# A differential-attention kernel: bit operations in VectorE's exponential, a bias tile in ScalarE's, and 222 shares for 204

## The reference

```python
scores = einsum('bhtd,bhsd->bhts', q * hd ** -0.5, k)   # 32 heads, 2048 x 2048, four batches
attn_w = softmax(scores, axis=-1)
aw = attn_w[:, :, 0] - lam * attn_w[:, :, 1]
attn = einsum('bhts,bhsd->bhtd', aw, v)                  # then RMS norm, subln_w, Wo
```

## Time and profile before

| | us |
|---|---|
| median of 3 runs | 3611.6 (3609.43 to 3613.68) |
| the profiled execution | 3607.35 |
| its span, first to last instruction | 3605.5 |
| ScalarE busy | 3534.4 (98%) |
| of that in the loop's exponentials | 3497.4 |
| TensorE busy | 3405.9 (94%) |
| VectorE busy | 2588.9 (72%) |
| GpSimd busy | 338.0 (9%) |
| mean granted TensorE clock | 0.998 |

### The profile page before, as it was taken

The page is one execution under the profiler, slowest core; times in us unless marked ns, Lnnn a source line. Parts: engine busy times, 40 slices in busy tenths (PEclk is TensorE's granted clock), DMA queues, the critical chain, the costliest instruction groups (busy, mean ns, idle before and its releaser), DMA issues. The chain is left out here.

```text
span 3605.5 us, 76890 instructions
## 1 busy us (share of the span) xinstructions
PE 3405.9 (94%) x32302; PEld 799.1 (22%) x32302; DVE 2588.9 (72%) x3808; ACT 3534.4 (98%) x2808; POOL 338.0 (9%) x229
## 2 busy tenths in 40 slices
PE   8999999999899999999999999999999999989998
PEld 5222112122122222222222222222221222211222
DVE  6687878863578687776367768677547888878886
ACT  5999999999999999999999999999999999999998
POOL 3010101010010100101001010100100000000001
PEclk9999999999999999999999999999999999999999
DMA  6111110111101111101111001111012110010000
GB/s 196 28 32 39 32 31 22 35 39 33 38 21 42 48 35 40 50 23 33 36 47 50 25 31 36 40 49 36 20 31 63 45 37 22 17 30 16 20 22 26
DMA packets 103700, 136.90 MB, mean 38 GB/s; under 512 B 9916, under 2 KB 88716, under 8 KB 103340
## 3 DMA queue, kind: packets, MB, share of 16 engines
q1 hardware_dynamic: 102524, 131.01, 12.9%
q10 hardware_dynamic: 816, 0.79, 0.1%
HBM read 72.50 MB, written 59.19 MB: 37 GB/s over the span
## 5 line engine op out<-in xcount | busy, mean ns | idle before, releaser
L1146 ACT ACTIVATE probs<-ps 128x1536 f32<-128x1536 f32 (+1 forms) x2732 | 3497.4, 1670 | 15.5 <-PE ps L1263 13.9
L1291 PE MATMUL ps<-probs,values 128*32 128x512 f32 x14600 | 2047.9, 606 | 4.9 <-DVE wmod_sb L1644 2.4
L1263 PE MATMUL ps<-queries,keys 25*128 25x512 f16 x7680 | 1003.9, 385 | 160.6 <-ACT probs L1146 142.0
L1263 PEld LDWEIGHTS ps<-queries,keys 25*128 25x128 f16 x7680 | 249.8, 91 | 1947.3 <-ACT probs L1146 1861.5
L1291 PEld LDWEIGHTS ps<-probs,values 128*32 128x32 f32 x14600 | 300.2, 108 | 416.9 <-issue 410.5
L1623 DVE TENSOR_SCALAR d_y<-ps 128x512 f32<-128x512 f32 x240 | 165.6, 690 | 295.4 <-PE ps L1263 284.7
L1708 DVE STREAM_TRANSPOSE seg_t<-ps 128x512 f32<-128x512 f32 x127 | 91.0, 716 | 356.9 <-PE ps L1291 356.4
L1060 POOL TENSOR_TENSOR seg_rs<-seg_ms,neg_half 128x16 f32<-128x16 f32 x64 | 185.7, 2901 | 1506.1 <-DVE seg_ms L1721 1506.1
L1640 DVE SCALAR_TENSOR_TENSOR wmod_sb<-wmod_sb 128x1024 f32<-128x1024 f32 x204 | 249.6, 1224 | 6.3
L1644 DVE SCALAR_TENSOR_TENSOR wmod_sb<-wmod_sb,gates 128x1024 f32<-128x1024 f32 x204 | 249.5, 1223 | 6.0
L1642 DVE SCALAR_TENSOR_TENSOR wmod_sb<-wmod_sb,d_y 128x1024 f32<-128x1024 f32 x204 | 249.3, 1222 | 5.3
(11 more groups left out here) (181 smaller groups left out, 1690.9 us busy)
## 6 DMA issues: line engine op xcount, KB each, us to landing
v_scr<-a_v SPq DMA_DIRECT2D x16, 1024.0 KB, 5.6
values<-v_scr SPq DMA_DIRECT2D x29, 512.0 KB
queries<-q_scr SPq DMA_DIRECT2D x116, 96.0 KB
keys<-k_scr SPq DMA_DIRECT2D x116, 96.0 KB
e_x<-in_x_dram SPq DMA_DIRECT2D x18, 512.0 KB, 5.2
attn_scr<-seg_o SPq DMA_DIRECT2D x254, 32.0 KB
e_attn<-attn_scr SPq DMA_DIRECT2D x31, 256.0 KB, 3.6
out_dram<-e_y SPq DMA_DIRECT2D x15, 512.0 KB, 3.3
```

The source lines that it names most:

```text
L1146: nc.scalar.activation(probs[:, s % PRING, at, :], ps[:, base + at.start:base + at.stop:at.step, :], ACT.Exp, scale=1.0 / SQUARE).then_inc ...
L1263: last = nc.tensor.matmul(ps[:, score_bank(n), :], keys[buf][at, u * P:(u + 1) * P], queries[buf][at, tc * CH:(tc + 1) * CH], start=True, ...
L1291: last = nc.tensor.matmul(pv[row:row + VW, :], values[buf][:, n % SEG_BANKS // HEADS, j // 2, :], probs_of(n), start=(i == 0), stop=(i == ...
```

## The change

Three things are changed together.

1. **VectorE's exponential.** The read now multiplies by log2(e) x 2^23 and writes int32, so that the bits of the result are split into a whole and a fractional part. A share then has six instructions instead of seven: two bit operations of the kind TENSOR_SCALAR, and four SCALAR_TENSOR_TENSOR for a polynomial of degree 6 in all. Before there were two TENSOR_SCALAR and five SCALAR_TENSOR_TENSOR. The result comes out eight times as large.
2. **ScalarE's exponential** has to carry the same factor. It gets `bias=eight[:, 0:1]`, log 8 in a new 128 x 1 tile that GpSimd sets at the start, on every one of the 2732 ACTIVATEs.
3. **The plan.** `shared(k)` compares with 8 instead of 5: 18 segments have two shares instead of one, 222 shares in all and 444 slots. They are segments 25 and 26 of the first batch, and 1, 2, 9, 10, 17, 18, 25 and 26 of the second and the third. `SHARE_COST` has the six parts.

```diff
-POLY = [-2.135305643081665, 4.020981311798096, 4.626499652862549, -0.9490653276443481]
-SHIFT = 1.2185084819793701
...
-ROUND = 1.5 * 2.0 ** 21
-QUARTER_LOG2E = float(np.log2(np.e) / 4.0)
+POLY = [-0.9341297723814943, 2.4233820625103575, 5.176821583615651, 1.7852414559499343]
+POLY_SCALE = 0.2812099198503226
+EIGHT = float(np.log(8.0))
+WHOLE_BITS, PART_BITS, PART_SIGN = 0x7F800000, 0x007FFFFF, -0x41800000
...
+LOG2E_BITS = float(np.log2(np.e) * 2.0 ** 23)
...
-    D_LINKS = 6
+    D_LINKS = 5
...
-        return 2 if sum(light.get(step, 3) for step in steps) <= 5 and not normed else 1
+        return 2 if sum(light.get(step, 3) for step in steps) <= 8 and not normed else 1
...
-    SHARE_COST = (695, 1230, 695, 1225, 1225, 1225, 1225)
+    SHARE_COST = (695, 695, 1225, 1225, 1225, 1225)
...
+            nc.gpsimd.memset(eight[:, :], EIGHT).then_inc(eight_set, 1)
...
+            act.wait_ge(eight_set, 1)
             for s in range(ALL_SLOTS):
...
-                nc.scalar.activation(probs[:, s % PRING, at, :], ps[:, base + at.start:base + at.stop:at.step, :], ACT.Exp, scale=1.0 / SQUARE).then_inc(exp_done, 1)
+                nc.scalar.activation(probs[:, s % PRING, at, :], ps[:, base + at.start:base + at.stop:at.step, :], ACT.Exp, bias=eight[:, 0:1], scale=1.0 / SQUARE).then_inc(exp_done, 1)
...
-                V.tensor_scalar(block_y(j)[:, half * CH:(half + 1) * CH], ps[:, score_bank(n), :], EXP_LOW * SQUARE, QUARTER_LOG2E / SQUARE, ALU.max, ALU.mult).then_inc(d_read, 1)
+                V.tensor_scalar(block_y(j)[:, half * CH:(half + 1) * CH].bitcast(I32), ps[:, score_bank(n), :], EXP_LOW * SQUARE, LOG2E_BITS / SQUARE, ALU.max, ALU.mult).then_inc(d_read, 1)
...
-                    link.then(V.tensor_scalar(d_n, y, ROUND, -ROUND, ALU.add, ALU.add))
+                    link.then(V.tensor_scalar(d_n.bitcast(I32), y, WHOLE_BITS, WHOLE_FLIP, ALU.bitwise_and, ALU.bitwise_xor))
                 elif part == 1:
-                    link.then(V.scalar_tensor_tensor(d_y[:, :], d_n, SHIFT, y, ALU.subtract, ALU.subtract))
+                    link.then(V.tensor_scalar(d_y[:, :].bitcast(I32), y, PART_BITS, PART_SIGN, ALU.bitwise_and, ALU.bitwise_or))
                 elif part == 2:
-                    link.then(V.tensor_scalar(d_n.bitcast(mybir.dt.int32), d_n, BIAS, 2.0 ** 25, ALU.add, ALU.mult))
+                    link.then(V.scalar_tensor_tensor(d_y[:, :], d_y[:, :], POLY[0], d_y[:, :], ALU.add, ALU.mult))
                 elif part == 3:
-                    link.then(V.scalar_tensor_tensor(out, d_y[:, :], -POLY[0], d_y[:, :], ALU.add, ALU.mult))
+                    link.then(V.scalar_tensor_tensor(out, d_y[:, :], POLY[1], d_y[:, :], ALU.add, ALU.mult))
                 elif part == 4:
-                    link.then(V.scalar_tensor_tensor(out, out, POLY[1], out, ALU.add, ALU.mult))
-                elif part == 5:
                     link.then(V.scalar_tensor_tensor(out, out, POLY[2], d_y[:, :], ALU.add, ALU.mult))
                 else:
-                    V.scalar_tensor_tensor(out, out, -POLY[3], d_n, ALU.add, ALU.mult).then_inc(d_done, 1)
+                    V.scalar_tensor_tensor(out, out, POLY[3], d_n, ALU.add, ALU.mult).then_inc(d_done, 1)
```

More of the change, by code:

```diff
@@ L13 @@
 F16 = mybir.dt.float16
+I32 = mybir.dt.int32
 P = 128
-POLY = [-2.135305643081665, 4.020981311798096, 4.626499652862549, -0.9490653276443481]
-SHIFT = 1.2185084819793701
-LEAD = 1.3595123291015625
-BIAS = (126.0 + LEAD) / 4.0 - 64.0
-ROUND = 1.5 * 2.0 ** 21
-QUARTER_LOG2E = float(np.log2(np.e) / 4.0)
+POLY = [-0.9341297723814943, 2.4233820625103575, 5.176821583615651, 1.7852414559499343]
+POLY_SCALE = 0.2812099198503226
+EIGHT = float(np.log(8.0))
+WHOLE_BITS, PART_BITS, PART_SIGN = 0x7F800000, 0x007FFFFF, -0x41800000
+WHOLE_FLIP = 0x40000000 | int(np.float32(POLY_SCALE).view(np.int32)) & PART_BITS
+LOG2E_BITS = float(np.log2(np.e) * 2.0 ** 23)
 EXP_LOW = -87.0
@@ L341, in put @@
                 due = GROUP_SLOT.get(next(g for g in range(entry[1] // SEG_BANKS * NB, ALL_SEGS * NB) if entry[1] in group_banks(g)), ALL_SLOTS)
-                later.extend((due, 0, SHARE_COST[part], ("share", share, part)) for part in range(7))
+                later.extend((due, 0, SHARE_COST[part], ("share", share, part)) for part in range(6))
             elif entry[0] == "evacuate" and entry[1] == "a" and 2 <= entry[3] < 6:
@@ L467, in adaln_diff_attention @@
         neg_half = sb("neg_half", [P, 16])
+        eight = sb("eight", [P, 1])
         wq, wk, wv, wo, wf = (sb(f"w_{n}", [P, EC, E]) for n in ("q", "k", "v", "o", "f"))
@@ L609, in adaln_diff_attention @@
         consts_set = sem("consts_set")
+        eight_set = sem("eight_set")
         c_loaded = sem("c_loaded")
@@ L1062, in _ @@
                         held.append(task)
-                    elif what == "share" and task[1] == 6:
+                    elif what == "share" and task[1] == 5:
                         shares = task[0] + 1
@@ L1628, in share_part @@
                 j = share - SHARES[k]
-                link, y, out = Chain(dve, d_chain, share * D_LINKS + part), block_y(j), d_blocks[j]
+                link, y, out = Chain(dve, d_chain, share * D_LINKS + part), block_y(j).bitcast(I32), d_blocks[j]
                 if part == 0:
                     dve.wait_ge(d_read, 2 * (share + 1))
-                    link.then(V.tensor_scalar(d_n, y, ROUND, -ROUND, ALU.add, ALU.add))
+                    link.then(V.tensor_scalar(d_n.bitcast(I32), y, WHOLE_BITS, WHOLE_FLIP, ALU.bitwise_and, ALU.bitwise_xor))
                 elif part == 1:
-                    link.then(V.scalar_tensor_tensor(d_y[:, :], d_n, SHIFT, y, ALU.subtract, ALU.subtract))
+                    link.then(V.tensor_scalar(d_y[:, :].bitcast(I32), y, PART_BITS, PART_SIGN, ALU.bitwise_and, ALU.bitwise_or))
                 elif part == 2:
-                    link.then(V.tensor_scalar(d_n.bitcast(mybir.dt.int32), d_n, BIAS, 2.0 ** 25, ALU.add, ALU.mult))
+                    link.then(V.scalar_tensor_tensor(d_y[:, :], d_y[:, :], POLY[0], d_y[:, :], ALU.add, ALU.mult))
                 elif part == 3:
-                    link.then(V.scalar_tensor_tensor(out, d_y[:, :], -POLY[0], d_y[:, :], ALU.add, ALU.mult))
+                    link.then(V.scalar_tensor_tensor(out, d_y[:, :], POLY[1], d_y[:, :], ALU.add, ALU.mult))
                 elif part == 4:
-                    link.then(V.scalar_tensor_tensor(out, out, POLY[1], out, ALU.add, ALU.mult))
-                elif part == 5:
                     link.then(V.scalar_tensor_tensor(out, out, POLY[2], d_y[:, :], ALU.add, ALU.mult))
                 else:
-                    V.scalar_tensor_tensor(out, out, -POLY[3], d_n, ALU.add, ALU.mult).then_inc(d_done, 1)
+                    V.scalar_tensor_tensor(out, out, POLY[3], d_n, ALU.add, ALU.mult).then_inc(d_done, 1)
                     dve.wait_ge(d_done, share + 1)
```

## The result

The changed kernel takes 3841.6 us (median of 4, 3836.87 to 3844.03) against 3612.4 of the kernel before (median of 4). The ratio is 1.0634, 95% interval 1.0616 to 1.0653: slower by 6.3%. Forecast were 3835 us in a range of 3788 to 3862.

What follows compares the result with a forecast made beforehand. The prediction took ScalarE's chain of loop exponentials as the bound. From 3607.35 us it took 15.5 for narrow slots, added 246 for the operand and took 3 for TensorE: 3835 us, range 3788 to 3862.

Steps and rivals of the forecast that it cites:

- ScalarE as the bound: Loop: one chain of 2732 exponentials, 3497.4 us busy and 15.5 idle; changes to one ACTIVATE go nearly one for one into time.
- the operand: Loop exponentials on ScalarE: the bias as pointer operand adds 0.09 us to each of 2732, 246 us in all.
- The halving of the two-operand rows: ScalarE: ACTIVATEs with two pointer operands (bias and scale) cost 0.18 us more, so one operand was taken as 0.09.
- The narrow slots: ScalarE in the 18 added shares: 36 more slots with two banks instead of three, 0.43 us each, 15.5 us less.
- TensorE: Loop: 0.09 us more in each slot removes some short ScalarE waits for scores, 3 us of 15.5 taken off.
- The argument on the clock: TensorE: granted clock at the upper level in all 40 slices, even one where it is half busy; no reason for lower.
- VectorE at nothing: VectorE's shares: new arithmetic and 18 more shares, 111 us less to 124 more work, off the path; nothing booked.
- Rival C: The 18 changed segments: VectorE's reads come late, up to 2.3 us each, 41 us on top, 3876 us; chance 0.05.
- Rival A: Loop exponentials: the operand replaces slack between start and end, 0.076 us each, 208 us, 3796 us in all; chance 0.17.
- my own list: Signs in the later profile: wide exponentials' starts about 1.43 us apart as forecast, 1.42 for Rival A, 1.33 for Rival B.
- Rival B: Loop exponentials: the operand's fetch is hidden in the queue from 0.09 us overlap on, 3592 us, faster; chance 0.05.
- Rival D: Loop exponentials: a bias alone costs clearly other than half of two, 3753 us at 0.06 each, 3917 at 0.12; chance 0.06.

Runs made afterwards that it cites:

- e2: The kernel before, with the loop's exponential bias read from a 128x1 tile holding 0, same plan and shares; 3842.8 us, ratio 1.0650.
- e7: The kernel before, with bias 0 and scale 1/64 of the loop's exponentials both read from 128x1 tiles; 4090.6 us, ratio 1.1334.
- e1: The changed kernel with the loop's bias as constant log 8 instead of the tile; 3604.8 us against 3609.4 of the kernel before, ratio 0.9987.
- e3: The changed kernel with constant bias and old limit 5 (204 shares), leaving only the bit arithmetic; 3607.4 us, ratio 0.9994 to the kernel before.
- e5: The changed kernel with constant bias and 12 of the 18 added shares, none in segments 25 and 26; 3601.0 us against 3609.0, ratio 0.9980.
- e4: The kernel before with limit 8 instead of 5: 222 shares with the old seven-part arithmetic, no bias; 3618.4 us, ratio 1.0023.
- e8: The kernel before with the pointer bias (0) in every second slot and the constant in the others; 3719.8 us, ratio 1.0307.
- e6: The changed kernel with constant bias and only the six added shares in segments 25 and 26; 3613.3 us, ratio 1.0013 to the kernel before.

## Why the prediction was right, point by point

The measured 3841.6 us lie 7 us above the sum. Part of the nearness is luck: the increase was put at 227.5 us, the medians are 229.2 apart and the two profiled executions 236.7, and the terms below err to both sides.

**ScalarE as the bound** and **the operand** were right, and with them the sign and the size. The operand was booked at 0.09 us and 246 us in all; e2 measured 0.0879 and 240.1. The halving of the two-operand rows, the one choice that could not be checked ahead, is borne out by e2 for the bias and by e7 for the scale. The Trainium skill ("ScalarE: Activation LUTs", section "What ACT_TABLE_LOAD costs") had about 93 ns; the runs have 88 and 91. For neighbours back to back it gives one overlap, about 93 ns. The runs agree that the operand hardly changes it, but have it larger: the duration of one alone less the distance of the starts is 1.451 - 1.331 = 0.120 us before and 1.538 - 1.423 = 0.115 after.

**The narrow slots** were right as busy time (15.5 booked, 14.0 measured) and wrong as time. The step that failed is "I count all of it, since ScalarE is the chain everywhere". It is not so at the borders of the batches, nor everywhere between them: e1 has 13.6 us more idle time than e3. With the operand it is of the same size: the kernel after idles 24.1 us, and e2, with the old plan, 8.7.

**TensorE**, -3 us: the operand alone takes 6.8 us off the idle time, more than booked, and the plan puts 15.4 on. The latter is the same failed step, and accounts for the 9 us by which the sum (3835) missed the profiled execution (3844.0): idle time +11.6 against the booked, busy time -4.5 (226.0 more for 230.5), and 2.1 outside the loop. What also waited with the plan in the middle of the batches (e1 idles 1.1 us each in segment 22 of the second and the third, e5 too) was not taken apart. The argument on the clock misread a row: the slice in which an engine is half busy is ScalarE's, and TensorE has an 8 there. Nothing hung on it, since the mean clock after is 0.994 against 0.998; but slices of 90 us hide local falls, 0.79 in 1843 to 1851 us of the kernel before and 0.76 in 1966 to 1974 us of the kernel after.

**VectorE at nothing** was right as far as the arithmetic goes (e3: no difference; the bit operations at 0.69; 2474 us busy for about 2480). Rival C, reads late in the 18 segments, did not come in that form: ScalarE has no idle time in segment 33 of the kernel after. But a read came late at each border of two batches, outside those segments. ScalarE's waits behind it are 1.90, 3.16 and 3.30 us in the kernel after and 0.75, 1.52 and 1.35 in e2, so 4.7 of the plan's 15.4 us of idle time have VectorE as the last releaser. With the old share of seven parts the idle time is far larger (e4: 40.8 us, 26.5 above e3's), and TensorE waits 15.0 us for the ends of shares instead of 5.3.

**Rival A** had a true premise and a false conclusion. The starts came to 1.423 us apart, what A said, and by my own list that would have spoken for A. But the durations went on growing, by about 8 ns an instruction instead of 12.5, and the busy time rose by 0.088 each and not 0.076. The distance of the starts was a poor sign, the busy time is the price. **Rival B** is refuted by e2 and e8: with an overlap of up to 0.75 us (2.174 us, the longest of e2, less 1.423) nothing is hidden. **Rival D** is refuted by e2, where the bias alone costs 0.088 us, half of the 0.179 that e7 has for two.

## What to carry to other kernels

Where one engine is the chain and issues thousands of equal instructions, look at what each instruction reads before counting how many elements it is spared: here one 128 x 1 operand on 2732 ACTIVATEs cost over fifteen times what 36 narrow slots could bring (240.1 us against 15.5), and the same factor as a constant cost nothing that could be measured (e3). With the second engine 94% busy, the gain on the first was worth only what the second could follow: against the kernel before, the six shares ahead of the borders lost 4 us and the twelve others gained 8. So see, in the planner's table, where postponed work piles up, and leave the gain out there.

## What the runs showed of the hardware that was not expected

An ACTIVATE's start is no exact measure of its turn. In steady stretches the starts run ahead of the ends: 1.331 us apart while the durations grow by about 12.5 ns each (1925 to 2127 ns over 17), so that the ends are 1.343 us apart. That is the 1.345 us of busy time per wide one, and the price to reckon with.

Pauses of 0.85 and 1.33 us of TensorE at a batch's border were followed in e1 by a granted clock of 0.57 over 8 us. The same pauses are not followed by it every time: with 0.92 and 1.33 us in e6, 0.79 and 1.33 in e4 and 0.81 and 1.43 in the kernel after, the 8 us behind the same border had 1.00, as in e3 and e5, where the last slot held one piece. What decides it was not found. The slot's overload is paid for more than once in any case: 2.20 us at once and 1.7 more at VectorE's next read in e1, with 1.8 us for the clock on top.
